# ScalarE empties the even transposes' bank directly behind the exponentials, ahead of its copy of transposed probabilities

## What is computed

```
h   = _ln(x, ln1_g, ln1_b) + shift
qkv = (h @ Wqkv.T).reshape(b, n, 3, H, HD)
q   = _ln(q, qn_g, qn_b)          # over the 64 features of a head
k   = _ln(k, kn_g, kn_b)
v   = qkv[:, :, 2]
scores = einsum('bhnd,bhmd->bhnm', q, k) / sqrt(HD)
attn   = softmax(scores, axis=-1)
o      = einsum('bhnm,bhmd->bhnd', attn, v)
x      = x + o @ Wout.T
```

## Time and profile before

| What | Before |
|---|---|
| Time, median of 3 runs | 1466.72 us (1466.05 to 1467.21) |
| The profiled execution's own time | 1464.1 us |
| Its span, first to last instruction | 1462.3 us |
| Mean granted TensorE clock | 0.989 |
| TensorE busy (matmuls) | 1376.4 us, 94% |
| ScalarE busy | 1038.9 us, 71% |
| VectorE busy | 960.8 us, 66% |
| GpSimd busy | 913.1 us, 62% |

### The profile page before, as it was taken

One profiled execution on the slowest core, in us unless ns is written; L12 is line 12 of the kernel. 1 busy time (PEld: TensorE's weight loads), 2 busy tenths in 40 slices (PEclk: granted clock), 3 DMA queues, 4 the chain that ended last, 5 costly groups with the idle time before them and its releaser, 6 DMA issues. The chain is left out here.

```text
span 1462.3 us, 30429 instructions
## 1 busy us (share of the span) xinstructions
PE 1376.4 (94%) x10795; PEld 1178.4 (81%) x10795; DVE 960.8 (66%) x2191; ACT 1038.9 (71%) x2703; POOL 913.1 (62%) x855
## 2 busy tenths in 40 slices
PE   7899999998899999999999999999999889899997
PEld 5799999996677787787787777787778678889896
DVE  5877767645666566567666667667656568678763
ACT  5566666547888888888888888878888742466662
POOL 2676676543767867776776776876786730364633
PEclk9899999999999999999999999999999999999999
DMA  5432222110100110110110010010011028144622
GB/s 156 132 106 73 66 68 72 48 38 21 37 29 9 51 44 9 52 44 9 51 52 22 31 51 23 31 51 33 20 44 38 23 71 332 35 111 122 168 34 29
DMA packets 61638, 89.04 MB, mean 61 GB/s; under 512 B 6144, under 2 KB 50992, under 8 KB 58800
## 3 DMA queue, kind: packets, MB, share of 16 engines
q1 hardware_dynamic: 53232, 75.82, 16.0%
q0 software_dynamic: 6144, 8.39, 3.5%
q10 hardware_dynamic: 2112, 2.88, 0.6%
HBM read 61.90 MB, written 25.18 MB: 60 GB/s over the span
## 5 line engine op out<-in xcount | busy, mean ns | idle before, releaser
L1382 POOL TENSOR_TENSOR prob<-prob,share_p 128x512 f32<-128x512 f32 x256 | 271.5, 1067 | 229.3 <-DVE share_p L1489 228.7
L1483 DVE TENSOR_REDUCE shift<-bank 128x2 f32<-128x512 f32 x256 | 164.6, 684 | 251.3 <-PE bank L1103 251.1
L1258 ACT ACTIVATE prob<-bank,shift 128x256 f32<-128x256 f32 x512 | 235.7, 474 | 87.0 <-DVE shift L1483 86.9
L147 PE MATMUL bank<-wqkv_h,rowsT_h 128*128 128x512 f32 x384 | 159.0, 414 | 2.8 <-PEq L311 1.7
L147 PE MATMUL bank<-wqkv_h,rowsT_l 128*128 128x512 f32 x384 | 150.9, 393 | 0.0
L147 PE MATMUL bank<-wqkv_l,rowsT_h 128*128 128x512 f32 x384 | 150.8, 393 | 0.0
L1115 PE MATMUL bank<-ident,prob 128*128 128x128 f32 x1024 | 142.5, 281 | 1.3 <-POOL prob L1382 1.3
L1370 POOL TENSOR_TENSOR landing<-landing,rq 128x512 f32<-128x512 f32 x128 | 132.0, 1052 | 8.4 <-DVE rq L1437 8.4
L1130 PE MATMUL bank<-pT,landing 128*64 128x256 f32 x1024 | 126.2, 386 | 1.2 <-ACT pT L1340 1.2
L1115 PEld LDWEIGHTS bank<-ident,prob 128*128 128x128 f32 x1024 | 109.3, 141 | 21.7 <-POOL prob L1382 4.2
L1196 PE MATMUL bank<-ident,landing 128*128 128x128 f32 x512 | 79.2, 278 | 34.4 <-ACT landing L1282 31.9
(11 more groups left out here) (324 smaller groups left out, 4528.2 us busy)
## 6 DMA issues: line engine op xcount, KB each, us to landing
landing<-in_fc1s SPq DMA_DIRECT2D x6, 1024.0 KB, 4.9
landing<-in_fc2s SPq DMA_DIRECT2D x6, 1024.0 KB, 5.0
rows<-in_x SPq DMA_DIRECT2D x16, 256.0 KB, 3.0
xT<-in_xT SPq DMA_DIRECT2D x16, 256.0 KB, 2.7
x_again<-in_x SPq DMA_DIRECT2D x16, 256.0 KB, 2.7
x_rows<-x SPq DMA_DIRECT2D x16, 256.0 KB, 3.2
rows<-x_rows SPq DMA_DIRECT2D x16, 256.0 KB, 3.1
x<-x_rows SPq DMA_DIRECT2D x16, 256.0 KB, 2.8
```

The lines of the kernel that those rows point to most:

```text
L147: last = nc.tensor.matmul(out, a, b, start=(n == 0), stop=(n == 3 * len(ks) - 1))
L1258: last = nc.scalar.activation(prob[at][:, n, :], score_bank[side][:, n * T:(n + 1) * T], ACT.Exp, bias=shift[:, at, n:n + 1], scale=-1.0, ...
L1382: nc.gpsimd.tensor_tensor(prob[at][:, :, :], prob[at][:, :, :], share[:, at, :].unsqueeze(2).to_broadcast([P, TT, T]), ALU.mult).then_inc( ...
L1483: nc.vector.tensor_reduce(shift[:, s % 2 * 2 + side, :], score_bank[side][:, :].rearrange("p (n m) -> p n m", n=TT), AX, ALU.min).then_inc ...
```

## The change

ScalarE's call that empties the even group is moved in its pair: it now stands directly behind the exponentials, ahead of the copy of transposed probabilities and ahead of the high parts. One pair of the program keeps the old place (`late`: pair 7 of step 14), since there the group itself needs a high part first. TensorE, VectorE, GpSimd and SyncE have the same instructions in the same order as before, and ScalarE has the same instructions with one moved in pairs 1, 4, 5 and 6 of a step. No semaphore and no wait is added or taken away.

```diff
                         for n in range(TT):
                             if live(t + 1) and s == SEED_PAIR[n]:
                                 seeds(t + 1, n)
+                        late = t == LAST_NEAR[0] and s == PAIRS - 1
                         if live(t):
                             exps(t, s)
+                        if not late:
+                            empty(*fill_at(t, 2 * s), 1 - odd)
                         b, q, _ = pair_at(t, s, 1, odd)
                         if live(b):
                             wait(act, pT_done, H, b, 2 * q + 1)
                             wait(act, pv_done, PAIRS, b, q - 1)
                             nc.scalar.activation(pT[q % 2 * 2][:, :, :].rearrange("p m n -> p (m n)"), pT_bank[0][:, :], ACT.Copy).then_inc(pT_act, 1)
-                        late = t == LAST_NEAR[0] and s == PAIRS - 1
                         high_parts(t, s, range(7 if late else 8), odd)
-                        empty(*fill_at(t, 2 * s), 1 - odd)
                         if late:
+                            empty(*fill_at(t, 2 * s), 1 - odd)
                             high_parts(t, s, (7,), odd)
                         for c, j in chunks_at(t, s):
                             if live(c):
```

## The result

| | Before | After | Forecast |
|---|---|---|---|
| Median | 1466.38 us (1464.22 to 1467.21, 4 runs) | 1432.52 us (1430.52 to 1433.95, 4 runs) | 1433.0 us, 1428.5 to 1443 |
| Ratio | | 0.977 (95%: 0.9753 to 0.9788) | 0.977 |
| Span of the profiled execution | 1462.3 us | 1428.7 us | |
| TensorE busy | 1376.4 us, 94% | 1370.5 us, 96% | |
| ScalarE busy | 1038.9 us, 71% | 1035.6 us, 72% | |

The changed kernel is 33.9 us faster. Run again later it came to 1430.65 us beside 1464.77 for the kernel before, ratio 0.9767 (0.9755 to 0.9780). One execution of each in that second set took far longer (2215.62 and 7441.04 us); the ratio leaves these two out.

A forecast was written before the change was run, and what follows sets the result against it. TensorE sets the pace, waiting 31.9 us for ScalarE's emptying. Gains of 28.6 (full steps), 1.7 (step 0), 1.2 (step 14) and 2.3 (h) sum to 33.8 us, giving 1433.0 us, range 1428.5 to 1443.

The forecast's parts named there:

- The fourth rival: No change: TensorE gives back in pairs 7 and 0 what it wins in pairs 4 to 6; 1466.7 us, chance 0.04.
- The second rival: Only the idle bracketed in the profile as TensorE's waits comes back, 24.0 us; 1442.7 us, chance 0.10.
- some 8: TensorE's waits for the emptying fall from 31.9 us to some 8: 3.7 ahead of step 0, about 0.3 a step.
- The hand-back in pair 6: New wait at pair 6's even group for pair 5's odd emptying: 0.27 us and 0.03 with it, 0.30 handed back.
- The first rival: Pair 5's odd emptying doesn't move, since VectorE or GpSimd sets its exponentials' start; 1.73 us a step, 1439.4 us, chance 0.10.
- The group h: Pair 1: emptying h earlier removes 0.19 us of unbracketed wait ahead of the gates in 12 steps, 2.3 us.
- 2.20 + 0.19: Gain of a full step: 2.20 us from pairs 4 to 6, 0.19 from the gates' hidden wait in pair 1.
- Step 14: Step 14 has the waits of pairs 4 and 5 and gains 1.2 us.
- the copy into pT comes later, cost 0: The copy comes one emptying later, 0.66 us in pairs 4 to 6, and delays no reader: cost 0.
- the products with the values would wait no more than before: Sign in the changed profile: TensorE's products with the values show no more wait for the copy into pT.
- My 0.59 and 0.85 us: Time to spare between the later copy into pT and the products with the values, in pairs 4 and 6.
- the third rival: Slower: the delayed copy into pT holds up TensorE; decided beyond 0.59 us extra delay; 1473.2 us, chance 0.04.

The follow-up runs named there:

- The kernel with h alone: Kernel before, with only the emptying of group h in pair 1 moved early; 1461.63 us beside 1464.92, ratio 0.9977.
- pair 5 alone: Kernel before, with only pair 5's even emptying moved up behind the exponentials; 1452.93 us beside 1466.45, ratio 0.9907.
- Half the move: Kernel before, with the even emptying of pairs 5 and 6 moved up past one high part only; 1450.59 us beside 1464.92, ratio 0.9905.
- the third experiment: Changed kernel, with the even emptying between the copy into pT and the high parts; 1433.12 us beside 1464.77, ratio 0.9781.
- the last: Changed kernel, with pair 5's odd emptying between the value chunks and, in step 14's pair 6, the copy into pT ahead of the even emptying; 1426.54 us, ratio 0.9731.
- the experiment with the copy last: Changed kernel, with the copy into pT behind the high parts and the chunks in pairs 4 and 6; 1448.99 us beside 1464.92, ratio 0.9888.
- h in its old place: Changed kernel, with group h of pair 1 emptied at its old place, only pairs 4 to 6 early; 1433.49 us beside 1464.77, ratio 0.9789.

## Why the prediction was right

**The start and the direction.** TensorE bounded the steps, the waits belonged to the even emptying, and the gap to the last exponential was long enough: no scores, transposes of probabilities or products of a full step wait for something new. The fourth rival (what is won in pairs 4 to 6 is given back in pairs 7 and 0) fell with the length of the step, 2.51 us shorter.

**The size of a wait.** The starts were right and the brackets too small. The second rival gave 1442.7 us. The kernel with h alone has every bracket and is 0.23% faster, and pair 5 alone brought 0.91 us and more for a bracket of 0.83. (Half the move can't tell the two readings apart: it shortens both by the same 0.52 us.) The difference between the forecast's time and this rival's is 9.7 us. The Trainium skill (Perfetto Trace Analysis, Per-engine timelines) says a TensorE end is computed. By the same reading the sign "some 8" us of waits for the emptying was wrong: 3.7 came, since the new small wait in pair 6 has no bracket either.

**The hand-back in pair 6** was there, 0.26 us and 0.03 in the group, for 0.30. The first rival (the odd emptying does not move) fell: the idle of 0.97 us in front of pair 5's exponentials is still 0.97.

**The group h** was undersized: 0.19 us in twelve steps, and it was 0.27 at the place itself (0.23 to 0.30 by the lengths of steps). I counted the start of the gates but not that they run 0.08 us shorter up to the next scores when they need not wait. This is most of the 0.12 us by which a full step gained more (2.51) than the forecast (2.20 + 0.19).

**Step 14** was oversized: 1.2 us forecast, 0.74 came (47.15 to 46.41 us). This is where "the copy into pT comes later, cost 0" failed, and with it the sign that the products with the values would wait no more than before: that wait grew from 1.2 to 1.6 us, all of it here. In that pair 6 no chunks stand between the transposes and the products with the values, so nothing covers the copy. TensorE's second eight products there, before and after:

```profile
1146.31 1.08 PE L1130 MATMUL bank<-pT,landing 128*64 128x256 f32 x8 [0.76 <-ACT pT L1340]
```

```profile
1111.19 1.08 PE L1130 MATMUL bank<-pT,landing 128*64 128x256 f32 x8 [1.24 <-ACT pT L1343]
```

0.48 us more, of 1.22 us that had been gained ahead of it (from the step's start to the first eight products, 37.10 us before and 35.88 after). Up to there the forecast 1.2 was right. Where the emptying is put behind the copy, the step takes 45.75 us (the third experiment) and with the copy first in this pair alone 45.76 (the last). I had taken a full step for all steps.

**To spare in pairs 4 and 6.** My 0.59 and 0.85 us were too small by the first eight products, 0.94 us. It did not touch the forecast, since the term was 0 either way, but the third rival's point of decision was wrong: its price would have fallen due only 1.5 us late, not 0.59. What an instruction costs by standing behind others shows in the experiment with the copy last, at 1.02 us of recorded wait a step; in the change itself it costs only in step 14. That ScalarE's queue is first in, first out, as the page on PSUM in the Trainium skill has it (PSUM — Partial Sum Buffer, Engine vs sequencer instructions), agrees with this: the copy was done behind the chunks that stand ahead of it.

**Where the sum met by luck.** Up to the start of step 15 the changed kernel is 35.1 us ahead (1154.52 to 1119.40), 1.3 more than the forecast; at the end of the span it is 33.6 ahead. The 1.5 us between are given back in the tail, in which both kernels have the same instructions. So the forecast came within 0.5 us of the median because errors met: the full steps and steps 0 and 1 gained some 1.8 us more than forecast, step 14 gained 0.5 less, and the tail took 1.5 that no term had. Over the twelve profiles of this case the stretch from step 15's start to the end takes 307.7 to 309.5 us. It is 307.8 in the kernel before, and 309.3 and 309.2 in the two profiles of the changed one. Why it differs stays open.

## What to carry to other kernels

Price a wait of TensorE by the distance between starts, compared with the same two lines where nothing waits, and look for distances that are too long without a bracket. When an emptying is moved up on an in-order engine, name what it passes and its first reader in every place where the pattern is broken (here the step without chunks), and follow the chain to the next emptying, which hands a part back. A pair of gains on one engine's order is not a sum: measure them together and apart.

## What the runs showed of the hardware that I had not expected

The granted clock of TensorE is not the same in equal work. Two windows of 4.5 us, from the same transposes of probabilities in step 14 on, across the start of step 15: the changed kernel, then the one with h in its old place; the columns are those of the earlier trace rows:

```profile
1117.80:1122.30 4.50, 3.90 (x33) 2.55 (x33) 3.01 (x7) 3.77 (x13) 4.50 (x5) 1.00 0.00 0
```

```profile
1121.00:1125.50 4.50, 4.48 (x28) 2.85 (x28) 2.12 (x5) 3.83 (x12) 4.50 (x5) 0.62 0.00 0
```

The first is at 1.00 of 2.4 GHz, the second at a mean of 0.62, so the larger part of it ran at 1.2 GHz. Eight products with the values took 1.97 us there instead of 1.08. TensorE had the same waits ahead in both, 1.37 and 1.38 us in front of the scores and 0.22 and 0.21 in front of the transposes. The kernel with pair 5 alone has such a dip in the same place. Whether a stretch is caught does not follow the edit in any way that I could see. What a dip costs in the end can't be told from it: from step 14's start to the end of the span the kernel with h in its old place takes 355.5 us and the changed one 355.7.

A longer distance is not always the clock. Behind step 15 the distance from one x2 group to the next is 8.13 us in the kernel before and 8.52 in the changed one, in both at a granted clock of 1.00 up to that group. The 0.39 us are a longer wait for VectorE, here before and after:

```profile
1196.13 0.66 PE L1201 MATMUL bank<-ident,x 128*128 128x128 f32 x4 [0.67 <-DVE x L1507]
```

```profile
1161.40 0.66 PE L1201 MATMUL bank<-ident,x 128*128 128x128 f32 x4 [1.05 <-DVE x L1509]
```

When the changed kernel was run again, the distance was 9.23 us with 1.77 of wait, and the tail all the same no longer.
